# Attention and mixture-of-experts kernel: column tiles for the weighted values, softmax sums over pairwise added tiles, inverse by DMA, residual two units behind

## What is computed

```python
def _L0_xattn_ref(q, k, v):            # 8 heads of the 512 sequence positions, ALPHA = 5
    qn = _l2norm(qh, axis=-2)
    kn = _l2norm(kh, axis=-2)
    qk = ALPHA * jnp.einsum('bhdq,bhdk->bhqk', qn, kn)
    sm = jax.nn.softmax(qk, axis=-1)
    out = jnp.einsum('bhqk,bhdk->bhdq', sm, vh)

def _L0_ffn_ref(x, Wg, bg, W1, W2):    # 4 experts, the best 2 per token, 512 tokens per expert
    logits = flat_x @ Wg + bg
    top_vals, top_idx = jax.lax.top_k(logits, TOPK)
    probs = jax.nn.softmax(sparse, axis=-1)
    for i in range(E):
        sel_p, sel_idx = jax.lax.top_k(score, capacity)
        h = jax.nn.gelu(flat_x[sel_idx] @ W1[i], approximate=False)
        out = out.at[sel_idx].add(h @ W2[i] * p)

x = x + _L0_xattn_ref(_layernorm(x, axis=-1), ctx_2048, ctx_2048)
x = x + _L0_ffn_ref(_layernorm(x, axis=-1), L0_ffn_Wg, L0_ffn_bg, L0_ffn_W1, L0_ffn_W2)
```

## Time and profile before

| what | us |
|---|---|
| median of 3 runs (653.88 to 655.61) | 655.24 |
| the profiled execution | 656.28 |
| its span | 654.3 |
| attention units, about | 0 to 231 |
| selection up to the experts' first matmul, about | 231 to 282 |
| experts, about | 282 to 654 |

### The profile page before, as it was taken

The page is one execution under the profiler, slowest core; times in us unless marked ns, Lnnn a source line. Parts: engine busy times, 40 slices in busy tenths (PEclk is TensorE's granted clock), DMA queues, the critical chain, the costliest instruction groups (busy, mean ns, idle before and its releaser), DMA issues.

```text
span 654.3 us, 8188 instructions
## 1 busy us (share of the span) xinstructions
PE 592.0 (90%) x2714; PEld 430.6 (66%) x2714; DVE 368.6 (56%) x638; ACT 300.4 (46%) x454; POOL 175.3 (27%) x139
## 2 busy tenths in 40 slices
PE   1899999999999951299999999999999999999994
PEld 1555555556555541168888888888888888888883
DVE  4678888888888878453425463434734245533312
ACT  2577776777678633044343332434333333434310
POOL 4544445445543600220021051040230120320002
PEclk9999999999999965579999999999999999999998
DMA  4423112221120023133333344151262332451001
GB/s 120 134 79 112 65 64 80 82 94 64 66 95 33 34 81 111 47 87 126 119 105 98 128 145 176 64 189 67 99 221 84 121 116 99 159 190 67 0 1 64
DMA packets 39636, 63.62 MB, mean 97 GB/s; under 512 B 3520, under 2 KB 20032, under 8 KB 39616
## 3 DMA queue, kind: packets, MB, share of 16 engines
q1 hardware_dynamic: 35776, 50.78, 22.7%
q0 software_dynamic: 3840, 12.59, 5.8%
HBM read 50.77 MB, written 12.58 MB: 97 GB/s over the span
## 4 chain that ended last, share of the span: by engine, by line
PE 73%; DVE 15%; issue 4%; POOL 1%; DMA 1%; DVEq 0%; ACT 0%; POOLq 0%
PE two L1299 28%; PE four L1329 9%; PE four L1328 9%; PE four L1326 9%; PE two L1168 9%; DVE p_inv L762 4%; PE four L1158 4%; PE bank_t L1185 1%; DVE o_norm L770 1%; PE bank_t L1137 1%; DVE junk L938 1%; PE bank_m L1145 1%; DVE x_all L772 1%; PE bank_t L1177 1%; DVE ss L723 1%
## 5 line engine op out<-in xcount | busy, mean ns | idle before, releaser
L677 ACT ACTIVATE h_f<-two 128x512 f32<-128x512 f32 x64 | 38.2, 598 | 231.7 <-PE two L1299 231.7
L1168 PE MATMUL two<-prob,v_t 128*128 128x512 f32 x256 | 116.7, 598 | 0.0
L1098 DVE TENSOR_TENSOR h_lo<-h_f,h_hi 128x512 fp32r<-128x512 f32 x64 | 44.1, 689 | 126.1 <-ACT h_hi L678 126.1
L1299 PE MATMUL two<-xt_hi,w_hi 128*128 (+1 forms) x256 | 103.0, 402 | 0.7 <-issue 0.7
L1299 PE MATMUL two<-xt_hi,w_lo 128*128 (+1 forms) x256 | 101.3, 396 | 0.0
L1299 PE MATMUL two<-xt_lo,w_hi 128*128 (+1 forms) x256 | 100.9, 397 | 0.0
L1329 PE MATMUL four<-w_hi,h_lo 128*128 128x512 f32 x256 | 100.5, 393 | 0.0
L1326 PE MATMUL four<-w_hi,h_hi 128*128 128x512 f32 x256 | 100.5, 392 | 0.0
L1328 PE MATMUL four<-w_lo,h_hi 128*128 128x512 f32 x256 | 100.4, 392 | 0.0
L1069 DVE TENSOR_TENSOR w_lo<-raw,w_hi 128x2048 fp32r<-128x2048 f32 x30 | 68.7, 2291 | 23.3 <-ACT w_hi L610 23.3
L582 ACT ACTIVATE prob<-four,rnorm 128x512 f32<-128x512 f32 x128 | 79.5, 695 | 2.3 <-PE four L1158 1.1
(11 more groups left out here) (167 smaller groups left out, 758.2 us busy)
## 6 DMA issues: line engine op xcount, KB each, us to landing
raw<-in_L_ffn_W SPq DMA_DIRECT2D x64, 512.0 KB, 3.9
x_all<-in_x SPq DMA_DIRECT2D x16, 256.0 KB, 2.7
c_sb<-in_ctx SPq DMA_DIRECT2D x16, 256.0 KB, 2.8
out<-x_all SPq DMA_DIRECT2D x16, 256.0 KB, 2.0
x2n_dram<-x2n SPq DMA_DIRECT2D x16, 256.0 KB, 2.1
cst<-in_consts SPq DMA_DIRECT2D x1, 354.5 KB, 4.8
x_got<-x2n_dram,idx_all POOLq DMA_INDIRECT x16
o_got<-out,idx_all POOLq DMA_INDIRECT x16
```

The source lines that it names most:

```text
L677: nc.scalar.activation(h_f[m % 2][:, :], z_ps[m % 2][:, :], ACT.Gelu)
L1098: nc.vector.tensor_tensor(h_lo[m % 2][:, :], h_f[m % 2][:, :], h_hi[m % 2][:, :].bitcast(F32), ALU.subtract).then_inc(h_split, 1)
L1168: last = nc.tensor.matmul(o_ps[h][:, :], v_t[u[1]][:, t, 2 * h:2 * h + 2, :] .rearrange("p a d -> p (a d)"), prob[h][t][:, :], start=(t == ...
L1299: return nc.tensor.matmul(z[:, :], w_part[c][:, w], x_k, start=start, stop=stop)
```

## The change

- The weighted values of the two heads go to the two column halves of the array: 64 columns of weights each, head 0 to partitions 0 to 63 of one bank, head 1 to partitions 64 to 127. The ones among the values are gone.
- The sums: the exponentials' tiles 0 and 1, and 2 and 3, are added first, for head 1 on VectorE and for head 0 on GpSimd (`half_sums`); two matmul pairs with ones as weights (64 columns) sum the results into the other bank (`sums`), already spread over 64 rows.
- The inverse: ScalarE copies the sums to SBUF (`take_sums`). SyncE moves one row of each head to 128 x 8 (`spread_inverse`), VectorE inverts these (`invert_few`), SyncE stores them and loads them back spread over 64 rows. The last unit inverts in full, from PSUM.
- The residual and x2n are two units behind instead of one, the router three instead of two; o_sb, p_inv and the small tiles of the norms are doubled.
- The orders of all engines within a unit are new. EARLY is 12. `first_low` is cut into eight parts, most of them timed by the selection's rounds.

```diff
+            def spread_inverse(u):
+                n = number(u)
+                sp.wait_ge(sum_taken, n + 1)
+                for h in range(2):
+                    half = slice(h * P // 2, (h + 1) * P // 2)
+                    sp.dma_start(few[half, :], p_sum[DH * h:DH * h + 1, :]).then_inc(few_in, 16)
+                sp.wait_ge(few_done, n + 1)
+                sp.dma_start(inv_dram.rearrange("(p j) -> p j", j=FEW), few_inv[:, :]).then_inc(few_out, 16)
+                sp.wait_ge(few_out, 16 * (n + 1))
+                for h in range(2):
+                    sp.dma_start(p_inv[u[1]][DH * h:DH * (h + 1), :],
+                                 inv_dram[D * h:D * (h + 1)].rearrange("(a d) -> a d", a=1).broadcast_to([DH, D])
+                                 ).then_inc(inv_in, 16)
...
             with sp.Fori(2, end) as h:
                 load_next((h, 1))
+                spread_inverse((h - 2, 1))
+                store_unit((h - 2, 0))
+                load_next((h + 1, 0))
+                spread_inverse((h - 1, 0))
                 store_unit((h - 2, 1))
-                load_next((h + 1, 0))
-                store_unit((h - 1, 0))
...
GpSimd, unit:
+                for h in POOL_HEADS:
+                    if ahead:
+                        pool.wait_ge(rq_ready, n + 2)
+                    half_sums(u, 0, h, behind > 0)
                 if ahead:
                     if behind:
-                        pool.wait_ge(exp_done, TT * number(u))
+                        pool.wait_ge(exp_done, TT * n)
                     key_norms(after(u))
+                for h in POOL_HEADS:
+                    if ahead > 1:
+                        pool.wait_ge(xsq_done, n + 3)
+                    half_sums(u, 1, h, behind > 0)
                 if ahead > 1:
-                    key_remainders(after(after(u)))
                     query_norms(after(after(u)))
-                if behind:
-                    finish(before(u))
                 if ahead > 2:
                     prepare(after(after(after(u))))
+                if behind > 1:
+                    finish(before(before(u)))
+                if ahead > 1:
+                    if behind > 1:
+                        pool.wait_ge(x2n_done, n - 1)
+                    key_remainders(after(after(u)))
...
VectorE, unit:
+                if ahead > 2:
+                    statistics(after(after(after(u))))
...
+                if ahead:
+                    queries(after(u), after(after(u)) if ahead > 1 else None)
+                    sum_key_squares(after(u))
+                for h in DVE_HEADS:
+                    half_sums(u, 0, h, behind > 0)
+                if behind:
+                    invert_few(before(u))
+                if ahead > 1:
+                    sum_query_squares(after(after(u)))
...
+                for h in DVE_HEADS:
+                    half_sums(u, 1, h, behind > 0)
...
+                if behind > 1 and ahead:
+                    residual(before(before(u)))
+                if behind > 1 and ahead:
+                    statistics_x2(before(before(u)))
+                if ahead > 1:
+                    widen_queries(after(after(u)))
+                if behind > 2:
+                    take_logits(before(before(before(u))))
+                if behind > 1 and ahead:
+                    normalize_x2(before(before(u)), behind > 3)
...
TensorE:
                 for h in range(2):
-                    if reused:
-                        pe.wait_ge(o_taken[h], number(u))
-                    last = nc.tensor.matmul(o_ps[h][:, :], v_t[u[1]][:, t, 2 * h:2 * h + 2, :]
-                                            .rearrange("p a d -> p (a d)"), prob[h][t][:, :],
+                    last = nc.tensor.matmul(o_ps[0][DH * h:DH * (h + 1), :], v_t[u[1]][:, t, h, :], prob[h][t][:, :],
                                             start=(t == 0), stop=(t == TT - 1))
...
+            def sums(u, behind, ahead):
+                for h in range(2):
+                    pe.wait_ge(halves_done[h], 2 * (number(u) + 1))
+                if behind:
+                    pe.wait_ge(sum_taken, number(u))
+                for n in range(2):
+                    for h in range(2):
+                        last = nc.tensor.matmul(o_ps[1][DH * h:DH * (h + 1), :], cst[:, C_ONES:C_ONES + DH],
+                                                half_sum[h][n][:, :], start=(n == 0), stop=(n == 1))
+                last.then_inc(sums_ready, 1)
...
ScalarE, unit:
+                if behind:
+                    take_sums(before(u), behind > 1)
+                if ahead:
+                    square_keys(after(u), behind + 1)
+                    take_v(after(u), behind + 1)
                 exponentials(u, 2, behind > 0)
...
-                nc.scalar.activation(p_sum[0:DH, :], o_ps[0][DH:P, :], ACT.Copy)
-                nc.scalar.activation(o_sb[0:DH, :], o_ps[0][0:DH, :], ACT.Copy).then_inc(o_taken[0], 1)
-                nc.scalar.activation(p_sum[DH:P, :], o_ps[1][0:DH, :], ACT.Copy).then_inc(sum_taken, 1)
-                nc.scalar.activation(o_sb[DH:P, :], o_ps[1][DH:P, :], ACT.Copy).then_inc(o_taken[1], 1)
+                nc.scalar.activation(o_sb[u[1]][:, :], o_ps[0][:, :], ACT.Copy).then_inc(o_taken, 1)
```

More of the change, by code:

```diff
@@ L190, in xattn_moe_kernel @@
             stats = att("stats", [P, 6])
[L191 to L193 removed]
+            mv = [att(f"mv{n}", [P, 2]) for n in range(2)]
+            var_e = [att(f"var_e{n}", [P, 1]) for n in range(2)]
+            rstd = [att(f"rstd{n}", [P, 1]) for n in range(2)]
             pad = att("pad", [P, 1])
@@ L337, in run_units @@
             unit((1, 0), 2, 3)
[L338 to L343, removed]
+            unit((1, 1), 3, 3)
+            with engine.Fori(2, last - 1) as h:
+                unit((h, 0), 4, 3)
+                unit((h, 1), 4, 3)
+            unit((last - 1, 0), 4, 3)
+            unit((last - 1, 1), 4, 2)
+            unit((last, 0), 4, 1)
+            unit((last, 1), 4, 0)
         def run_experts(engine, expert):
@@ L636, in unit @@
                     exponentials(after(u), 1, True)
-                if ahead in (1, 2):
-                    split_hi(0, 2 - ahead)
-                take_o(u, behind > 0)
+                if ahead > 1:
+                    round_keys(after(after(u)), True)
+                if not ahead:
+                    for c in range(AHEAD):
+                        split_hi(0, c)
+                take_o(u, behind > 1)
             run_units(act, unit)
-            take_x2t((UNITS // 2 - 1, 0))
+            take_x2t((UNITS // 2 - 2, 1))
             act.wait_ge(key_set, 1)
@@ L815, in _ @@
             widen_queries((0, 1))
-            def unit(u, behind, ahead):
-                if ahead:
-                    queries(after(u), after(after(u)) if ahead > 1 else None)
-                    sum_key_squares(after(u))
-                if behind:
-                    invert_sums(before(u))
-                if ahead > 1:
-                    sum_query_squares(after(after(u)))
-                if behind:
-                    residual(before(u))
-                    statistics_x2(before(u))
-                if ahead > 2:
-                    statistics(after(after(after(u))))
-                if behind:
-                    normalize_x2(before(u), behind > 2)
-                if ahead > 1:
-                    widen_queries(after(after(u)))
-                if behind > 1:
-                    take_logits(before(before(u)))
-            run_units(dve, unit)
-            end = (UNITS // 2 - 1, 1)
             done = [0]
@@ L906, in _ @@
                                     ).then_inc(thr_done, 1)
+            residual(before(end))
+            statistics_x2(before(end))
             invert_sums(end)
-            take_logits(before(end))
-            residual(end)
+            normalize_x2(before(end), True)
+            take_logits(before(before(end)))
+            residual(end, 1)
             statistics_x2(end)
             normalize_x2(end, True)
+            take_logits(before(end), bank_m)
             early = EARLY * P
@@ L1225, in unit @@
                     transpose_queries(after(after(u)))
+                if behind > 2:
+                    if ahead:
+                        pe.wait_ge(v_taken, n + 2)
+                    else:
+                        pe.wait_ge(logit_done, n - 3)
+                    transpose_x2(before(before(before(u))))
                 if ahead:
@@ L1230, in unit @@
                     scores(after(u), 1, True)
-                if behind > 1:
-                    router_logits(before(before(u)))
+                if behind > 2:
+                    router_logits(before(before(before(u))))
                 weighted_values(u, 2)
                 weighted_values(u, 3)
+                sums(u, behind, ahead)
             run_units(pe, unit)
```

208 lines of the change are left out of this document (132 added, 76 removed).

## The result

| | before | after |
|---|---|---|
| median, us | 655.3 (653.88 to 655.61, 4 runs) | 670.77 (669.95 to 671.2, 4 runs) |
| span of the profiled execution, us | 654.3 | 668.1 |
| granted clock of TensorE, mean | 0.954 | 0.939 |

What follows compares the result with a forecast made beforehand. TensorE bounds the kernel before, VectorE little behind; after, VectorE's wait for x's load closes a 15.2 us round. Nine rounds +16.9, units 13 and 14 -3.2, end -2: +11.7, so 667 us, range 651 to 680.

Steps and rivals of the forecast that it cites:

- q_f of unit 4: Start of the kernel: pair gains in units 0 to 2 are given back to x's loads, q_f stays at 63.4.
- nine rounds: Units 4 to 13: each round goes from 13.32 to 15.2 us, together +16.9.
- from q_f of unit 13 to the last unit's scores: Units 13 and 14 load nothing, so TensorE's 11.5 us replaces 13.05 in each: -3.2.
- SyncE's queue: Load of x stands behind the store of x2n, VectorE's preceding operation: 3.5 us idle VectorE in units 3 to 12.
- The round: Through VectorE alone: q_f to x2n 10.6, load 3.55, statistics 1.04, together 15.2 us; upper bound 15.6.
- The exclusion: GpSimd's additions and VectorE's operations with two SBUF inputs exclude each other: round 15.2 us with it, 14.8 without.
- TensorE: Column tiles run in pairs, 24 records in 5.3 us; its unit falls from 12.9 to 11.5 us.
- The rule on weight loads: On TensorE, 24 half-width loads would stand bare: unit 13.9 us, about 657 us in the case without the wait; 2%.
- The ends: Start unchanged; units 13 and 14 -3.2; last unit to x2n -4, then +1.5 to 2, taken as -2; experts nothing.
- Rival 1: VectorE's wait for x is absent or hidden: round 11.7 us, -22, 633 us; chance 11%.
- Rival 4: TensorE's granted clock falls in the new pauses; part of a unit at half speed is hidden: 680 to 740; 6%.
- Rivals 2 and 3: 2: wait for x cheap, 653 to 657, 8%. 3: TensorE's column tiles don't run together, about +49, 704, 7%.

Runs made afterwards that it cites:

- x_ahead: The changed kernel with SyncE's load of x moved directly ahead of the stores of x2 and x2n: 638.4 us, ratio 0.9743 to before.
- stats_back: The changed kernel with the statistics of x put back behind the second statistics in VectorE's order, SyncE's order kept: 645.95 us, ratio 0.986 to before.
- old_stats_first: The kernel before with only the statistics of x moved first in VectorE's unit (small norm tiles doubled for it): 686.69 us, ratio 1.0484 to before.
- add_3_1: The changed kernel with the load of x ahead of the stores and three of the four additions on VectorE: 631.83 us, ratio 0.9649 to before.
- x_ahead_dve: The changed kernel with the load of x ahead of the stores and all four additions on VectorE: 634.7 us, ratio 0.9684 to before.

## Why the prediction was right, and where its sizes were off

Its sum, term by term, against the two traces (differences of after to before, us):

| term | predicted | measured |
|---|---|---|
| q_f of unit 4 | 0 | 62.25 - 63.37 = -1.1 |
| nine rounds | 9 x (15.2 - 13.32) = +16.9 | 9 x (15.67 - 13.32) = +21.2 |
| from q_f of unit 13 to the last unit's scores | -3.2 | 32.90 - 35.97 = -3.1 |
| from there to x2n of unit 15 | -4 | 19.76 - 22.79 = -3.0 |
| from there to the experts | +1.5 to 2 | 41.11 - 40.13 = +1.0 |
| experts | 0 | 371.0 - 372.2 = -1.1 |
| sum | +11.7 | +13.8, the difference of the spans |

(The last scores of after begin at 236.19, its x2n at 255.95, its experts at 297.06; in before the experts begin at 282.12. The medians lie 15.5 apart, 1.7 more than the spans.)

**SyncE's queue.** This is the step that decided, and it held: the wait stands where it was put, is released by what was named, and has the size of store, issue and landing. Without it the same kernel would have been faster than before (638.4), so the direction was no luck. x_ahead and stats_back each break the loop at one end and get 32 and 25 us; old_stats_first makes it in the old kernel.

**The round.** It is the mis-sized term, 0.47 too short, 4.2 us over nine. Most of it lies between q_f and the end of x2n: 10.6 was predicted, the two rounds shown have 152.19 - 140.98 = 11.21 and 167.36 - 156.64 = 10.72, 0.36 more in the mean. The wait, predicted as 3.5, has a mean of 3.67: 3.43 in one of them, and at the loop's turn 3.91, since the load there is issued 1.01 behind the store (167.38 to 168.39), not 0.67. GpSimd in the first of the two shows the rest:

```profile
144.57 2.07 POOL L468 TENSOR_TENSOR rnorm<-ss_max,power 128x8 f32<-128x8 f32 x1 [5.33 <-DVE ss_max L799]
146.61 1.80 POOL L501 TENSOR_TENSOR half_sum<-prob 128x512 f32<-128x512 f32 x1
148.38 2.10 POOL L468 TENSOR_TENSOR rnorm<-ss_max,power 128x8 f32<-128x8 f32 x1
150.44 1.07 POOL L468 TENSOR_TENSOR rstd<-var_e,power 128x1 f32<-128x1 f32 x2
```

The roots last 2.07 and 2.10 where 1.96 and about 2.0 were put in, and in five of the nine rounds, as in this one, GpSimd's addition starts beside an o_norm that is already under way: then it is the addition that is held (1.80 for 1.28), and after it x_all (1.53) instead of o_norm. The prediction had only the other case, o_norm held until the addition ends (162.28, 1.76), which it took from the earlier trace rows. Where the addition is the one held, all behind it on GpSimd comes 0.5 later, rstd2 and x2n too. The upper end of the prediction's range for the round, 15.6, said to have every collision paid, was too low for that.

**The exclusion.** It was used as the price of GpSimd's second addition. The Trainium skill, SBUF — State Buffer, SBUF: two separate sides, states that the two exclude each other for a whole instruction. o_norm at 1.76 beside an addition and at 0.69 without (add_3_1) bears it out, and so does the faster kernel with more work on VectorE. By that rule the sum was 15.2 and without it 14.8; measured is 15.67.

**TensorE.** 5.3 us for twelve pairs were predicted and 12 x 0.45 = 5.4 measured; its unit of 11.5 is borne out by its busy time in add_3_1, 102.84 / 9 = 11.43. The 12.9 that the prediction started from stands in none of its rows; TensorE's busy time in before is 117.80 / 9 = 13.09 a round. Nothing hung on that here, since TensorE sets no round of after. The rule on weight loads of the Trainium skill, TensorE: Matmul & The Clock Gate, Part 3, by which the loads of the column tiles would stand bare, isn't borne out. Two of the four starts of weight loads in the eight records of values from 154.41 (128 x 64 is the size of one load, x2 the two heads' loads, taken together):

```profile
154.89 0.14 PEld L1268 LDWEIGHTS two<-prob,v_t 128*64 128x64 f32 x2 [0.28 <-issue]
155.32 0.14 PEld L1268 LDWEIGHTS two<-prob,v_t 128*64 128x64 f32 x2 [0.28 <-issue]
```

Two loads, 0.14 together, begin every 0.43, the pace of the pairs of matmuls themselves; nothing is added to it.

**The ends.** The reciprocal of the last unit, the sums and the parts of the first low weights came to -3.1 - 3.0 + 1.0 = -5.1, where -5.2 to -5.7 was summed. The start gained 1.1, which the prediction gave back to the load of unit 5. These terms were read from the two traces and not tested one by one. Two errors of about a microsecond each, in the start and in the experts, hid half of the error in the round; that part of the agreement is luck.

**The rivals.** Rival 1 named 633 us for the case without the wait; the wait was there, and with it taken out (x_ahead) the time is 638.4, since a round of VectorE and GpSimd is 12.38 and not 11.7. Rival 4's half clock did come, in pieces, and by the waits it was hidden by the pauses, as its text says for a part of a unit. Rivals 2 and 3 didn't come.

## What to carry to other kernels

When an operation moves within an engine's order, write down for every transfer it waits for what stands ahead of that transfer in its queue: if it is a store of what the same engine makes just before, the two are a loop, and issue and landing are added to every round, however fast the rest becomes. Then price a helper engine by what its operations do to the neighbours, not by its idle time: an addition of 1.28 us on the idle GpSimd cost VectorE more than making it itself. And a stage that gains nothing from a faster engine is to be asked for its longest repeating wait first; here it was one line in the view of summed waits.

## What was unexpected of the hardware

- GpSimd's additions and VectorE's operations with two inputs in SBUF hold each other in turns. Where VectorE's comes second it ends 0.56 us behind the addition (o_norm from 162.28 to 164.04, the addition from 162.15 to 163.48). Where the addition comes second it ends 1.12 behind o_norm (146.61 to 148.41, o_norm from 146.60 to 147.29), and x_all in turn 0.55 behind the addition. VectorE's x_norm, one large input with a mean and a root per row, is held as well (0.96 us in mean in x_ahead, 0.55 undisturbed), while the reductions, the statistics and the reciprocal beside GpSimd's work kept their 0.63 to 0.70 and 0.20.
- GpSimd's roots over 128 x 8 last 2.08 us in the mean of after's nine rounds, where before had 1.65 and 1.96. In x_ahead_dve, with no addition on GpSimd at all, they last 2.10, so it isn't GpSimd's own additions. Whether it is VectorE's work beside them or something else was not tried.
- TensorE's granted clock fell from its upper to its lower level (2.4 to 1.2 GHz) inside several units of after, in rounds in which it was busy for 83% of the time and waited 2.6 us in the mean (3.5 at the longest) for x_norm; the scores' records behind the pause that ended at 158.61 were then 0.63 long and 0.43 apart instead of 0.39 and 0.23. In x_ahead, 95% busy in the same units, it stayed at 1.00.
